# Splitting the key weight by column halves at the start of a gated cross-attention and spiking MLP kernel

## What is computed

```python
x = x + jnp.tanh(g_xattn[0]) * _L0_xattn_ref(ctx_1024, _layernorm(x, axis=-1), Wq, Wkv, Wout, gm, bm, gl, bl)
x = x + jnp.tanh(g_ffn[0]) * _L0_ffn_ref(_layernorm(x, axis=-1), W_fc, W_proj)
...
xn = layernorm(x, gm, bm)          # here x is the context, 750 rows a batch
ln = layernorm(latents, gl, bl)    # latents: the 224 normalised rows of x
q = ln @ Wq
kv = jnp.concatenate([xn, ln], axis=-2) @ Wkv
k, v = jnp.split(kv, 2, axis=-1)
...                                # softmax attention, 8 heads of 64, then @ Wout
h = jnp.square(jax.nn.relu(x @ W_fc.T)); y = h @ W_proj.T
...                                # five steps of a leaky neuron with a threshold, mean of its spikes
```

## Time and profile before

| | |
|---|---|
| median of 3 runs | 1070.77 us (1070.26 to 1070.95) |
| profiled execution, its own time | 1070.37 us |
| its span in the trace | 1068.5 us |
| PE matmul busy | 1048.5 us, 98% of the span |
| PE weight load busy | 862.6 us, 81% |
| DVE / ACT / POOL busy | 747.2 / 592.7 / 307.4 us |
| granted TensorE clock, mean | 0.999 |

### The profile page before, as it was taken

One profiled execution on the slowest core, in us unless ns is written; L12 is line 12 of the kernel. 1 busy time (PEld: TensorE's weight loads), 2 busy tenths in 40 slices (PEclk: granted clock), 3 DMA queues, 4 the chain that ended last, 5 costly groups with the idle time before them and its releaser, 6 DMA issues.

```text
span 1068.5 us, 19370 instructions
## 1 busy us (share of the span) xinstructions
PE 1048.5 (98%) x7105; PEld 862.6 (81%) x7105; DVE 747.2 (70%) x1166; ACT 592.7 (55%) x1147; POOL 307.4 (29%) x284
## 2 busy tenths in 40 slices
PE   5999999999999999999999999999999999999997
PEld 5878778877887877887788788787788888998886
DVE  7378877867877787686796778759535555485766
ACT  5558447655655754765574576457446433445535
POOL 4333634335434353433444434343000000000000
PEclk9999999999999999999999999999999999999999
DMA  6302010101201101010120200013431000300111
GB/s 193 133 1 76 2 35 20 54 0 34 75 0 34 67 8 34 11 64 0 34 75 0 74 0 0 26 36 103 145 102 46 12 1 20 100 1 25 36 59 40
DMA packets 31891, 47.43 MB, mean 44 GB/s; under 512 B 2284, under 2 KB 11516, under 8 KB 31852
## 3 DMA queue, kind: packets, MB, share of 16 engines
q1 hardware_dynamic: 31716, 46.74, 13.6%
q10 hardware_dynamic: 136, 0.17, 0.1%
HBM read 39.56 MB, written 7.34 MB: 44 GB/s over the span
## 4 chain that ended last, share of the span: by engine, by line
PE 95%; DVE 3%; DMA 1%; issue 0%; SPq 0%; ACT 0%; DVEq 0%
PE work L477 41%; PE work L641 14%; PE score L654 13%; PE heads_out L593 9%; PE score L556 9%; PE score L492 2%; PE maxes L578 1%; PE maxes L568 1%; PE heads_out L605 1%; PE score L841 1%; DMA xin<-in_ctx 1%; PE heads_out L477 1%; DVE on L1403 0%; PE maxes L477 0%; PE work L624 0%
## 5 line engine op out<-in xcount | busy, mean ns | idle before, releaser
L1823 POOL TENSOR_TENSOR dsum<-dsum,probs 125x448 f32<-125x448 f32 x186 | 226.0, 1215 | 14.6
L477 PE MATMUL work<-wv,xT 128*125 128x512 f32 (+1 forms) x768 | 187.4, 398 | 0.0
L477 PE MATMUL work<-xT,wk 128*128 128x486 f32 (+2 forms) x768 | 183.9, 390 | 0.5 <-DVE kst L1368 0.5
L477 PEld LDWEIGHTS work<-wv,xT 128*125 128x125 f32 (+1 forms) x768 | 137.8, 183 | 36.7 <-issue 2.3
L641 PE MATMUL work<-zT,wf 128*128 128x512 f32 (+1 forms) x768 | 164.3, 364 | 0.1
L477 PEld LDWEIGHTS work<-xT,wk 128*128 128x128 f32 x768 | 140.2, 188 | 29.9 <-issue 4.6
L961 ACT ACTIVATE probs<-score 125x448 f32<-125x448 f32 (+1 forms) x256 | 119.9, 549 | 72.1 <-PE score L556 71.8
L641 PEld LDWEIGHTS work<-zT,wf 128*128 128x128 f32 x768 | 131.4, 189 | 23.1 <-issue 0.8
L1820 POOL TENSOR_TENSOR dsum<-probs 125x448 f32<-125x448 f32 x31 | 35.7, 1152 | 391.0 <-ACT probs L967 391.0
L1356 DVE TENSOR_TENSOR probs<-probs,maxes 125x1792 f32<-125x1792 f32 x64 | 128.2, 2014 | 5.7 <-PE maxes L578 5.2
L654 PE MATMUL score<-hT,wp 128*128 128x512 f32 (+1 forms) x576 | 117.4, 354 | 0.0
(11 more groups left out here) (190 smaller groups left out, 1424.9 us busy)
## 6 DMA issues: line engine op xcount, KB each, us to landing
xin<-in_ctx SPq DMA_DIRECT2D x42, 250.0 KB
neuron<-in_L_ffn_W_fc SPq DMA_DIRECT2D x16, 256.0 KB, 4.5
neuron<-in_L_ffn_W_proj SPq DMA_DIRECT2D x16, 256.0 KB, 2.8
xres<-in_x SPq DMA_DIRECT2D x16, 224.0 KB, 2.6
x_scratch<-xres SPq DMA_DIRECT2D x16, 224.0 KB, 2.4
xin<-in_x SPq DMA_DIRECT2D x14, 224.0 KB, 9.3
zt<-x_scratch SPq DMA_DIRECT2D x3, 1024.0 KB, 6.4
fin<-x_scratch SPq DMA_DIRECT2D x3, 1024.0 KB, 5.6
```

Source lines behind the costliest of these rows:

```text
L477: mm = pe.matmul(bank, lhs(i, k), rhs(j, k), start=(n == 0), stop=(n == len(passes) * chunks - 1))
L1823: pool.tensor_tensor(total[0:ROWS[t]], total[0:ROWS[t]], tile(t), ALU.add).then_inc(dchain if t < TILES - 1 else dsum_done, 1)
```

## The change

The key weight is loaded, split and waited for by column halves. Columns 0 to 255 (blocks c = 0 and 1) are one DMA of all 512 rows, 1 KB a row, where the first half was; columns 256 to 511 are a second one, behind pairs 2 and 3. ACT's and DVE's splits of the first half stay where the first two were, each piece two row blocks by 256 columns. ACT's high parts of the second half move behind its last `first_norm`, and POOL's low parts behind its last `first_norm`. They have a semaphore of their own, `wk_late`, for which SP waits before the value weight's load, and PE before the first product of block 2. PE's transposes of tiles 4 to 7 now wait for two low parts. On ACT's queue the four vectors go in front of the first end rows.

```diff
-            for i in range(2):
-                sp.dma_start(staged[0][:, 2 * i:2 * i + 2, :],
-                             Wkv[2 * i * P:2 * (i + 1) * P, 0:D].rearrange("(k p) n -> p k n", p=P)).then_inc(wk_in[i], 16)
+            def key_weight(i):
+                half = slice(i * D // 2, (i + 1) * D // 2)
+                sp.dma_start(staged[0][:, :, half], Wkv[:, half].rearrange("(k p) n -> p k n", p=P)).then_inc(wk_in[i], 16)
+
+            key_weight(0)
             first_pair(2)
             first_pair(3)
+            key_weight(1)
             load_weight(1, Wq, staged[1])
-            sp.wait_ge(w_lo[0], DC)
+            sp.wait_ge(w_lo[0], DC // 2)
+            sp.wait_ge(wk_late, DC // 2)
...
-            pe.wait_ge(w_lo[0], DC)
+            pe.wait_ge(w_lo[0], DC // 2)
             first_transposes(4, 5, 6, 7)
...
             keys_queries(0, 1, (2,), first=True)
+            pe.wait_ge(wk_late, DC // 2)
             keys_queries(0, 2, (0,), first=True)
...
+            def key_piece(a_, n):
+
+                return a_[:, 2 * (n % 2):2 * (n % 2) + 2, n // 2 * D // 2:(n // 2 + 1) * D // 2]
+
+            def key_hi(*ns):
+                for n in ns:
+                    act.wait_ge(wk_in[n // 2], 16)
+                    act.activation(key_piece(wk[:, 0], n), key_piece(staged[0], n), ACT.Copy).then_inc(w_hi, 1)
...
-            act.dma_start(xin[EVEN:CT, 0:4, :], first_tiles(0, 4)[EVEN:CT]).then_inc(ends_in[0], 16)
             for i, v in enumerate((gm, bm, gl, bl)):
                 act.dma_start(vectors[i * DC:(i + 1) * DC, :],
                               v.rearrange("(k p) -> k p", p=P)).then_inc(vec_in, 16)
+            act.dma_start(xin[EVEN:CT, 0:4, :], first_tiles(0, 4)[EVEN:CT]).then_inc(ends_in[0], 16)
...
             first_norm(0)
-            split_hi(0, wk, 0, 1)
+            key_hi(0, 1)
             first_norm(2)
-            split_hi(0, wk, 2, 3)
             hi_chunks(0, 0, 0, 1, 2, 3)
             first_norm(5)
             first_norm(7)
+            key_hi(2, 3)
             split_hi(1, wq, 0, 1)
...
-            split_lo(0, wk, 0, 1)
+            key_lo(0, 1)
             first_statistics(2)
...
             first_norm(3)
-            split_lo(0, wk, 2, 3)
             first_root_of(2)
             first_root_of(3)
             first_norm(4)
             first_norm(6)
+            key_lo(2, 3)
             split_lo(2, wv, 0, 1, 2, 3)
```

More of the change, by code:

```diff
@@ L233, in flamingo_block @@
         ends_in = [sem(f"ends_in{i}") for i in range(2)]
+        wk_late = sem("wk_late")
         pad_ready = sem("pad_ready")
@@ L1190, in split_hi @@
                 for k in ks:
[L1191 to L1194, removed]
+                    act.wait_ge(w_in[i], 16)
                     act.activation(w[:, 0, k, :], staged[i][:, k, :], ACT.Copy,
                                    scale=QSCALE if i == 1 else 1.0).then_inc(w_hi, 1)
+            def key_piece(a_, n):
[4 more added lines that the diff above has]
+                    act.activation(key_piece(wk[:, 0], n), key_piece(staged[0], n), ACT.Copy).then_inc(w_hi, 1)
             def take_row(ready, done):
@@ L1598, in batch, with key_piece, key_lo @@
                 gated_residual(b, 1)
+            def key_piece(a_, n):
+                return a_[:, 2 * (n % 2):2 * (n % 2) + 2, n // 2 * D // 2:(n // 2 + 1) * D // 2]
+            def key_lo(*ns):
+                for n in ns:
+                    dve.wait_ge(w_hi, n + 1)
+                    dve.tensor_tensor(key_piece(wk[:, 1], n), key_piece(staged[0], n),
+                                      key_piece(wk[:, 0], n).bitcast(F32), ALU.subtract).then_inc(w_lo[0], 1)
             def split_lo(i, w, *ks):
@@ L1874, in first_norm, with key_piece, key_lo @@
                                    ALU.mult, ALU.add).then_inc(ln_pool, 1)
+            def key_piece(a_, n):
+                return a_[:, 2 * (n % 2):2 * (n % 2) + 2, n // 2 * D // 2:(n // 2 + 1) * D // 2]
+            def key_lo(*ns):
+                for n in ns:
+                    pool.wait_ge(w_hi, n + 1)
+                    pool.tensor_tensor(key_piece(wk[:, 1], n), key_piece(staged[0], n),
+                                       key_piece(wk[:, 0], n).bitcast(F32), ALU.subtract).then_inc(wk_late, 1)
             def split_lo(i, w, *ks):
```

## The result

The changed kernel takes 1073.86 us (median of 13 runs, 1073.03 to 1074.28), the kernel before, run beside it, 1070.71 (13 runs, 1069.17 to 1072.34). The ratio is 1.003, with a 95% interval of 1.0021 to 1.0038: slower by 3.15 us (2.2 to 4.1). The profiled execution took 1073.88 us, 3.51 more than the profiled one of before (1070.37).

What follows compares the result with a forecast made beforehand. PE, 95% of the chain, was held at its start by pair 2's load and DVE's 0.9 us wait for POOL. A gain of 0.7 us and a splits' cost of 0.7 summed to 0: 1070.8 us, range 1068.9 to 1072.6.

Steps and rivals of the forecast that it cites:

- rival B: On ACT's queue, end rows come last, after SP's first five loads: 1071.8 to 1073.1 us; chance 0.23.
- E: Start of DVE's first statistics, gated by the end rows: 4.91 us before, forecast 7.0, bounds 4.9 and 9.3.
- a gain of 7.7 - E: How much earlier DVE's low parts of the first half of the tokens start: 0.7 us at E = 7.0.
- V = E + 9.4: V, start of DVE's low parts of the first half of the tokens (17.12 before), follows E by 9.4 us.
- a cap of 2.3 us on the gain: At E = 4.91 the key weight's first half, landing at 9.2, bounds V at 14.8: 2.3 us at most.
- Earlier vectors gain nothing themselves: On ACT's queue, vectors arriving sooner bring nothing, since DVE and ACT then wait for E's chain.
- POOL's wait inside nmu: In DVE's statistics of pair 2, 0.9 us of waiting for POOL's key-weight low parts disappears.
- The moved splits: Later key-weight splits on ACT and POOL delay DVE's low parts; PE waits 0.7 us, bounds 0 and 1.0.
- Pair 2's landing: On SP's queue, 512 KB less in front: lands at 10.9 us instead of 12.49, 0.2 charged for 1 KB rows.
- The value weight's load: Waits for POOL's late low parts, near 21.5 instead of 15.2 us; costed at nothing, 2 us of cover left.
- A: Rival: end rows are not late, E below 6, DMA engines taking turns between queues; 1068.5 to 1069.8 us, chance 0.22.
- C: Rival: load order brings nothing, one lagging DMA engine keeps pair 2 landing at 12.5; 1070.6 us, chance 0.05.

Runs made afterwards that it cites:

- the first experiment: The changed kernel with the first end rows again in front of the four vectors on ACT's queue; 1070.03 us, ratio 0.9998 to the kernel before.
- the old splits: The kernel before with only the four vectors put in front of the first end rows, splits unchanged; 1073.78 us, ratio 1.0033.
- the swapped ones: The first experiment with ACT's query-weight high parts before the key weight's second half, and the vector work moved later on ACT and DVE; 1068.59 us, ratio 0.9988.
- the run where PE's slow idle transposes came in between: The first experiment with ACT's first two query-weight high parts in front of the key weight's second half; 1069.67 us, ratio 0.9995.
- the last repetition: Unaltered rerun: end rows first, ACT's query-weight high parts before the key weight's second half, vector work later on ACT and DVE; 1068.82 us, ratio 0.9984.
- its repetition: The changed kernel run again unaltered; 1073.24 us, ratio 1.0029 to the kernel before.

## Why the prediction was wrong

Forecast 1070.8 us in a range of 1068.9 to 1072.6; measured 1073.86. The direction is rival B's, beyond its upper end.

**E, the term that failed.** I had put E at 7.0; it was 10.58, 3.6 us later, and 1.3 later than its upper bound. The step that failed is the time from the first end row's move to DVE's start, not the wait in front of it. The sum had the first row at 5.7, the middle of 4.4 and 7.0, and it moved at 6.13, 0.4 later. For the rest the sum had 1.5 us, the length of the window 2.0 to 3.5 in which the same 104 KB moved before, when SP's queue took 58% of the DMA engines and ACT's 24%, and it took off 0.2 because the vectors are issued early. The runs have 4.45 us there, from 6.13 to 10.58, so 3.2 of the 3.6 are in this term. Two things were missing from it. From the last row to DVE's start some 1.2 us pass (with two vectors in front the last row ended at 6.23, and E is 7.44); the upper bound had 0.8 for that, and the sum nothing. And the rows themselves move slowly then, in a full queue whose engines move 153 GB/s in 8 to 10 us: some 1.8 us.

That is the whole error: the recorded formula, a gain of 7.7 - E with the splits' 0.7, gives with E = 10.58 a loss of 3.6, or 1074.0 from the profiled 1070.37; the profiled execution was 1073.88. PE's first product started at 23.89, outside the 19 to 23.5 that I had named. That the start came out nearly right is in part luck: it was the middle of two rows of other transfers, and what the end rows wait for was known only after the experiments. Why the late transfer is slow stays open.

**V = E + 9.4** held: 19.87 - 10.58 = 9.29. With E = 5.20, where I had a cap of 2.3 us on the gain, V would have been 14.8; it was 15.86. I had overlooked that ACT waits for the vectors before it touches tile 0, so their arrival at 8.49 was the next thing late, and took 1.1 us of the cap. "Earlier vectors gain nothing themselves" was true of the changed kernel, where E was late, but not of the one in which it is not. With the work on the vectors out of the way V gained 2.45 in one profile and 1.82 in the other, near the cap of 2.3.

**POOL's wait inside nmu** went, 0.17 instead of 1.06 us.

**The moved splits** were costed at 0.7. In the changed kernel V is 2.85 late and the MLP's first product 3.5; in the first experiment V is 1.16 early and the MLP's first product 0.6. So about 0.6 is lost behind V in both. With the old splits it was nothing (2.60 against 2.6), with the swapped ones 0.05 (2.45 against 2.4), and 0.5 in the run where PE's slow idle transposes came in between (1.40 against 0.9). The cost was sized rightly. The low parts of tiles 4 to 7 began at V + 6.1, where I had V + 6.4. The Trainium skill, page "SBUF — State Buffer", section "SBUF: two separate sides", has a DVE operation with two SBUF inputs and a GpSimd operation that reads SBUF exclude each other for a whole instruction; the runs agree, 2.54 and 2.98 us side by side, 1.28 and 2.63 when almost apart.

**Pair 2's landing** was to be 10.9. The changed kernel's DMA issues in a window around 1.7 us and one around 2.2 (KB each, us from issue to landing):

```profile
vals<-in_L_xattn_Wkv SPq DMA_DIRECT2D x1, 512.0 KB, 9.6
...
xin<-in_ctx SPq DMA_DIRECT2D x1, 448.0 KB, 10.8
```

and those of the first experiment:

```profile
vals<-in_L_xattn_Wkv SPq DMA_DIRECT2D x1, 512.0 KB, 6.7
...
xin<-in_ctx SPq DMA_DIRECT2D x1, 448.0 KB, 7.9
```

Pair 2 landed at 2.23 + 10.8 = 13.0 in the changed kernel, and at 2.18 + 7.9 = 10.1 with the end rows first. With the end rows first the step was right to the better side, 2.4 us gained on 12.5 instead of 1.6 (1.7 in the profile of the last repetition), so the 1 KB rows cost nothing that shows. Not all of it is the order: with the second half in front again pair 2 landed at 11.6, 0.9 earlier than before. In the changed kernel the end rows land among SP's loads, and those, the key half too (11.3 instead of 8.4), come 3 us later, in its repetition 2. The two kernels differ in nothing but the order on ACT's queue, so the late end rows cost these 3 us and the new load order does not; by what, no run tells. It did not matter there, since DVE came to pair 2 only at 16.27.

**The value weight's load** was issued at 25.58, after POOL's late low parts, and I had costed it at nothing; ACT began to read it at 34.61 without a wait for it, so it did cost nothing.

**The rivals.** A, whose turns between the queues the Trainium skill's page "DMA: Bandwidth & Descriptors", section "Queues, rings and completion order", would give to each DMA engine, fell. With taking turns alone, an issue at 1.90 and nothing in front would not come 4.2 us later than one at 0.73, nor would moving SP's issues bring it back. Here the first end row moved 3.8 us after its issue, when SP's queue had moved 1.11 MB. Until 6 us ACT's queue moved 19 packets with 0.00 MB together, the vectors at most. B, with my 0.23, had the direction and half the mechanism: the end rows come behind SP's bulk, but not behind all of the loads issued before them, and its upper end fell short by the slow transfer. C fell too: pair 2 landed at 10.1 once the end rows were in front.

What stays open: what keeps the partial order between the two queues, the DMA engines or what hands them their work, and why the engines move half as much while the end rows come late. No run tells.

## What to carry to other kernels

On two queues that fill the same DMA engines, the order of issue across both counts: a small DMA that gates the first computation has to be issued before the other queue's bulk, and even four tiny DMAs in front of it can be too much, not by their bytes but by the microsecond and a half in which the other queue issues its loads. When a trace gives the duration of a transfer, look at how full the engines were while it ran: the end rows' 1.5 us of a stretch with idle engines had become over 3 in a full one. And when a bound is taken away, walk the chain of the next one to its root: here it led from the load of pair 2 to a wait for 8 KB of vectors. With that wait gone the kernel is 1.2 to 1.6 us faster than before, of which the new load order makes some 0.6. Last, read a clock of 1.00 only where the trace has a record of it; the rate of equal matmuls tells the rest.

## What was unexpected of the hardware

- A DMA of 104 KB issued by ACT 1.17 us later reached DVE 4.2 us later (E 5.20 and 9.36), and with SP's loads moved behind it by the same time only 1.0 later (6.20, when pair 0 landed).
- While the end rows, 13 partitions of 2 KB rows, moved late among SP's loads, the busy DMA engines moved 153 GB/s in 8 to 10 us instead of 294, and the key half landed 9.6 us after its issue instead of 6.7.
- DMAs of one queue overtook earlier ones of the other: the end rows, issued at 2.32, landed at 10.48; the key half, issued at 1.68, landed at 11.3.
- ACT's first activation in front of its DMAs did not hold their issue: the end rows were issued at 1.06 us, 0.33 later than without it, in the middle of ACT's table load (0.74 to 2.02).
- PE's 32 idle transposes took 5.03 us in one kernel and 3.69 in another. The rate doubled where the trace's record of the granted clock begins, at 16.5 us in the first and 12.95 in the second.
- At the end the granted clock fell to 0.50 before PE's last transposes in some runs and behind them in others, and with it 0.6 us of an earlier start was lost (first experiment) or next to nothing (1.8 us at the MLP's first product, 1.72 in the time, in the last repetition).
